# Two heads at a time in the row halves of the array, with fewer load slots

## The reference

```
layer 0: head size 32, scores = q k^T / sqrt(32) + causal mask - (pos_i - pos_j), gate silu(p) on the output
layer 1: head size 64, rotary q and k, four key/value heads shared by four query heads each
layer 3: head size 16, q and k from a low-rank projection
each:    o = softmax(scores) v, then the output projection
```

## Time and profile before

| | us |
|---|---|
| median of 3 runs | 4516.4 (4515.51 to 4525.6) |
| profiled execution | 4514.84 |
| its span | 4513.2 |
| PE busy, share of the span | 3375.2, 75% |
| DVE busy | 1985.5, 44% |
| ACT busy | 1256.6, 28% |
| mean granted TensorE clock | 0.866 |

### The profile page before, as it was taken

One profiled execution on the slowest core, in us unless ns is written; L12 is line 12 of the kernel. 1 busy time (PEld: TensorE's weight loads), 2 busy tenths in 40 slices (PEclk: granted clock), 3 DMA queues, 4 the chain that ended last, 5 costly groups with the idle time before them and its releaser, 6 DMA issues. The chain is left out here.

```text
span 4513.2 us, 51689 instructions
## 1 busy us (share of the span) xinstructions
PE 3375.2 (75%) x17778; PEld 1820.8 (40%) x17778; DVE 1985.5 (44%) x4344; ACT 1256.6 (28%) x1983; POOL 559.7 (12%) x610
## 2 busy tenths in 40 slices
PE   5799966777899567999974776855456887459676
PEld 2233333676555322333351454532332333222555
DVE  3466540432788654444413456223313774234212
ACT  3234421221354212333311300112112544224022
POOL 0101110000344231111100200001001001003100
PEclk9899988878899788999986978877687998679888
DMA  3302013112000232222222312223313111335243
GB/s 109 92 18 44 17 64 143 40 35 71 15 19 19 99 83 58 44 34 34 23 63 74 77 39 86 77 95 71 105 66 75 21 31 49 113 104 80 85 141 107
DMA packets 237902, 295.46 MB, mean 65 GB/s; under 512 B 69054, under 2 KB 182904, under 8 KB 235160
## 3 DMA queue, kind: packets, MB, share of 16 engines
q1 hardware_dynamic: 214360, 235.97, 18.1%
q0 software_dynamic: 23360, 57.11, 5.9%
HBM read 185.38 MB, written 104.73 MB: 64 GB/s over the span
## 5 line engine op out<-in xcount | busy, mean ns | idle before, releaser
L1007 DVE TENSOR_REDUCE l1a_nmax<-ps 128x1 f32<-128x512 f32 (+3 forms) x384 | 207.9, 556 | 219.6 <-PE ps L889 168.7
L2447 DVE SCALAR_TENSOR_TENSOR f_acc<-ps,f_gates,f_acc 128x256 f32<-128x256 f32 x672 | 278.0, 476 | 14.7 <-PE ps L2380 14.7
L991 ACT ACTIVATE l1a_probs<-ps 128x1024 f32<-128x1024 f32 x192 | 156.1, 813 | 379.8 <-PE ps L917 272.7
L2367 PE MATMUL ps<-f_x_parts,f_wf 128*128 128x512 f16 x1056 | 251.9, 382 | 7.5 <-DVE f_x_parts L2421 7.5
L1007 DVE TENSOR_REDUCE l0a_nmax<-ps 128x1 f32<-128x512 f32 (+3 forms) x384 | 200.9, 555 | 121.4 <-PE ps L889 92.5
L1007 DVE TENSOR_REDUCE l3a_nmax<-ps 128x1 f32<-128x512 f32 (+3 forms) x384 | 199.3, 553 | 80.7 <-PE ps L889 66.0
L991 ACT ACTIVATE l0a_probs<-ps 128x1024 f32<-128x1024 f32 (+1 forms) x192 | 145.5, 811 | 229.0 <-PE ps L917 181.4
L991 ACT ACTIVATE l3a_probs<-ps 128x1024 f32<-128x1024 f32 (+1 forms) x192 | 148.7, 809 | 184.1 <-PE ps L917 147.8
L2347 POOL TENSOR_TENSOR f_h_parts<-f_hid,f_h_parts 128x512 f16<-128x512 f32 x132 | 152.2, 1158 | 199.2 <-ACT f_h_parts L2400 199.2
L928 PE MATMUL ps<-l1a_probs,l_v_all 128*64 128x512 f32 (+3 forms) x768 | 166.7, 511 | 8.4 <-ACT l1a_sums L980 8.2
L889 PE MATMUL ps<-mask,ident_b 128*128 128x128 bf16 x768 | 169.5, 230 | 0.0
(11 more groups left out here) (696 smaller groups left out, 6457.9 us busy)
## 6 DMA issues: line engine op xcount, KB each, us to landing
f_w<-in_L_ffn_w_dram SPq DMA_DIRECT2D x16, 1024.0 KB, 7.2
x_qt<-x0p_st SPq DMA_DIRECT2D x16, 512.0 KB, 2.6
x0a_q<-x_qt SPq DMA_DIRECT2D x8, 1024.0 KB, 4.8
l1a_qs<-l_q_h SPq DMA_DIRECT2D x64, 128.0 KB
x3a_qs<-x_q_h SPq DMA_DIRECT2D x64, 128.0 KB
f_wf<-in_L_ffn_W_dram SPq DMA_DIRECT2D x99, 64.0 KB, 1.9
l0a_qs<-l_q_h SPq DMA_DIRECT2D x32, 128.0 KB
l0a_ks<-l_k_h SPq DMA_DIRECT2D x16, 256.0 KB
```

Of the source, the lines that this page charges most:

```text
L991: act.activation(probs[0:KR, n % SLOTS, 2 * pr:2 * pr + 2, 0:w], SB[x % 2][:, :, 0:w], ACT.Exp).then_inc(s_["exps"], 1)
L1007: dve.tensor_reduce(nmax[:, s % LEAD, f.chunk, f.p, f.tile:f.tile + f.n], src, AX.X, ALU.max, negate=True).then_inc(s_["maxed"], 1)
L2367: ins = pe.matmul(bank[i % 2], wf[:, s % 2, m, d * I:(d + 1) * I], x[:, d, g * GN:(g + 1) * GN], start=j == 0, stop=j == len(terms) - 1)
L2447: ins = dve.scalar_tensor_tensor(out=acc[:, t, :], in0=Y[i % 2][:, j, :], scalar=gates[:, t, ds(e + s, 1)], in1=acc[:, t, :], op0=ALU.mult ...
```

## The change

Three stacks are new, `TILED_32`, `TILED_64` and `TILED_16`, and the plans of the three attentions are paired. In the first pass heads are taken two at a time: the even head's q and k lie on partitions 0 to 63, the odd head's on 64 to 127, and each matmul uses its half of the rows. The two write to two banks; the mask matmuls of both follow, over the whole array. Only the high parts of q and k enter in layers 0 and 1 (38 and 64 rows). There the first pass has tiles of its own (`qa`, `ka`), loaded by 12 (layer 0) or 6 (layer 1) transfers ahead of the second-pass loads, with semaphores of their own (`a_ld`); `LOADS` becomes 2 there, and the two `SA` banks remain. In layer 3 the second pass is halved too: q and k have three parts per head on 48 rows plus the two rows of the maximum, both passes use the same tile, a load has 18 transfers and `maximum_rows` four; three `SA` banks, and one bank for the values instead of two; `LOADS` stays 3. `Plan.lay` hands out pairs instead of single maxima. SP's loop, quoted above, is unchanged.

```diff
+TILED_32 = Stack(32, STACK_32.q_parts, STACK_32.k_parts, [104], 38, 96, 102, 0, paired=True)
+TILED_16 = Stack(16, [(0, 0, "h"), (0, 16, "h"), (0, 32, "l")], [(0, 0, "h"), (0, 16, "l"), (0, 32, "h")], [64], 48, 32, 48, 0, q_fill=0.0, halved=True, paired=True)
+TILED_64 = Stack(64, STACK_64.q_parts, STACK_64.k_parts, [128, 128], 64, 64, 126, 1, q_fill=0.0, paired=True)
...
+            if self.paired:
+                n_max = len(todo) // 2 * 2
+                todo = [todo[i:i + 2] for i in range(0, n_max, 2)] + [[it] for it in todo[n_max:]]
+                cost = [0.3 + st.firsts[0].w / 450] * (n_max // 2) + [0.7] * (len(todo) - n_max // 2)
+            else:
+                todo = [[it] for it in todo]
...
-                beside[parts[-1][0]][parts[-1][1]].append(add(it))
+                    beside[n][k] += [add(it) for it in todo.pop(0)]
...
+                order = [(p + e, i) for p in range(0, G, 2) for i in range(gq) for e in range(2)] if paired else [(p, i) for p in range(G) for i in range(gq)]
...
-    LOADS = LEAD // 2 + 2
+    LOADS = 2 if stack.paired and not stack.halved else LEAD // 2 + 2
...
-    n_ld = len(stack.q_parts) * GB + len(stack.k_parts) + (GB + 1 if q_pos is not None else 0)
+    paired, halved = stack.paired, stack.halved
+    apart = paired and not halved
+    HB = 2 if halved else 1
+    n_ld = HB * (len(stack.q_parts) * GB + len(stack.k_parts)) + (GB + 1 if q_pos is not None else 0)
+    n_first = 2 * (GB + 1) * (2 if q_pos is not None else 1)
+    NSA = 3 if paired and own_sums else 2
...
-        qs = ph.sb("qs", [P, LOADS, C, GB, G, QC], F16)
-        ks = ph.sb("ks", [P, LOADS, KH, C, plan.n_keys], F16)
+        qs = ph.sb("qs", [P, LOADS, C, GB, G // HB, QC], F16)
+        ks = ph.sb("ks", [P, LOADS, KH // HB, C, plan.n_keys], F16)
+        KA = max(KH // 2, 1)
+        qa = ph.sb("qa", [P, LOADS, GB, G // 2, QC], F16) if apart else None
+        ka = ph.sb("ka", [P, LOADS, KA, plan.n_keys], F16) if apart else None
...
-        SA = [k.ps[:, i, :] for i in range(2)]
-        SB = [k.ps[0:KR, 2 + 2 * i:4 + 2 * i, :] for i in range(2)]
-        X = [k.ps[:, 6, :], k.ps[:, 7, :] if own_sums else k.ps[:, 6, :]]
+        SA = [k.ps[:, i, :] for i in range(NSA)]
+        SB = [k.ps[0:KR, NSA + 2 * i:NSA + 2 + 2 * i, :] for i in range(2)]
+        NX = 2 if own_sums and NSA == 2 else 1
+        X = [k.ps[:, 8 - NX if own_sums else 6, :], k.ps[:, 7, :] if own_sums else k.ps[:, 6, :]]
         Y = k.ps[:, 7, :]
-        NX = 2 if own_sums else 1
+        a_ld = [ph.sem(f"a_ld{i}") for i in range(LOADS)] if apart else ld
...
+                    if apart and tb >= LOADS:
+                        sp.wait_ge(s_["a_done"], turned_at[2 * (tb - LOADS) + 1])
+                    if q_pos is not None and tb < LOADS:
+                        sp.wait_ge(s_["k_filled"], slot + 1)
+                        sp.wait_ge(s_["q_filled"], slot + 1)
+                    for e in range(2 if apart else 0):
+                        rows = q["h"][h0 * dh:(h0 + G) * dh].rearrange("(h d) n -> d h n", d=dh)[:, e::2, :]
+                        k_rows = kk["h"][hk * dh:(hk + KH) * dh].rearrange("(h d) n -> d h n", d=dh)
+                        k_rows = k_rows[:, e::2, :] if KH > 1 else k_rows
+                        e0 = e * HALF
+                        for g in range(GB):
+                            sp.dma_start(qa[e0:e0 + dh, slot, g, :, :], rows[:, :, b * T + g * QC:b * T + (g + 1) * QC]).then_inc(a_ld[slot], 16)
+                        sp.dma_start(ka[e0:e0 + dh, slot, :, :], k_rows[:, :, b * plan.n_keys:(b + 1) * plan.n_keys]).then_inc(a_ld[slot], 16)
+                        if q_pos is not None:
+                            for g in range(GB):
+                                rows = q_pos[h0 + e:h0 + G:2, :, b * T + g * QC:b * T + (g + 1) * QC]
+                                sp.dma_start(qa[e0 + dh + 3:e0 + dh + 6, slot, g, :, :], rows.rearrange("h r n -> r h n")).then_inc(a_ld[slot], 16)
+                            sp.dma_start(ka[e0 + dh:e0 + dh + 3, slot, :, :], k_pos[h0 + e:h0 + G:2, :, b * T:(b + 1) * T].rearrange("h r n -> r h n")).then_inc(a_ld[slot], 16)
                     if tb >= LOADS:
                         sp.wait_ge(s_["b_done"], PR * plan.first_unit[2 * (tb - LOADS) + 2])
...
+                    for e in range(2 if halved else 0):
+                        e0 = e * HALF
+                        for c, r0, part in stack.q_parts:
+                            rows = q[part][h0 * dh:(h0 + G) * dh].rearrange("(h d) n -> d h n", d=dh)[:, e::2, :]
+                            for g in range(GB):
+                                sp.dma_start(qs[e0 + r0:e0 + r0 + dh, slot, c, g, :, :], rows[:, :, b * T + g * QC:b * T + (g + 1) * QC]).then_inc(ld[slot], 16)
+                        for c, r0, part in stack.k_parts:
+                            rows = kk[part][hk * dh:(hk + KH) * dh].rearrange("(h d) n -> d h n", d=dh)[:, e::2, :]
+                            sp.dma_start(ks[e0 + r0:e0 + r0 + dh, slot, :, c, :], rows[:, :, b * plan.n_keys:(b + 1) * plan.n_keys]).then_inc(ld[slot], 16)
+                    for c, r0, part in stack.q_parts if not halved else []:
...
+                        for e in range(2 if halved else 0):
+                            half = G * GQ // 2
+                            sp.dma_start(qs[e * HALF + R + i:e * HALF + R + i + 1, (s // 2) % LOADS, 0, st.q0 // QC, :, :],
+                                         m[e * half:(e + 1) * half, s % LEAD, :]).then_inc(m_ld[s % LEAD], 16)
+                        if halved:
+                            continue
...
+                    if halved:
+                        pool.memset(ks[stack.m0:HALF, i], 1.0)
+                    for e0 in (0, HALF) if q_pos is not None else ():
+                        pool.memset(ka[e0 + dh:e0 + dh + 6, i], 1.0)
+                    pool.memset(ks[P - HALF + stack.m0:P, i] if halved else ks[stack.m0:R + 2, i, :, stack.m_chunk, :], 1.0).then_inc(s_["k_filled"], 1)
...
-                            pe.wait_ge(s_["maxed"], a - 1)
+                            pe.wait_ge(a_ld[slot], 16 * (n_first if apart else n_ld) * (s // 2 // LOADS + 1))
+                        if a >= NSA:
+                            pe.wait_ge(s_["maxed"], a - NSA + 1)
                         f = st.firsts[i]
-                        for j in range(f.n):
+                        if paired:
+                            e0, g = (f.p % 2) * HALF, f.p // 2
+                            rows = slice(e0, e0 + stack.max_rows)
+                            left = qa[rows, slot, st.q0 // QC, g, f.tile * P:(f.tile + 1) * P] if apart else qs[rows, slot, 0, st.q0 // QC, g, f.tile * P:(f.tile + 1) * P]
+                            kg = g if KH > 1 else 0
+                            right = ka[rows, slot, kg, f.key:f.key + f.w] if apart else ks[rows, slot, kg, 0, f.key:f.key + f.w]
+                            ins = pe.matmul(sa[:, 0:f.w], left, right, start=True, stop=not f.masked)
+                            if f.masked and i % 2 == 0:
+                                return
+                            if f.masked:
+                                pe.matmul(SA[(a - 1) % NSA][:, f.w - P:f.w], k.ident_b[:], k.mask[:], start=False, stop=True).then_inc(s_["a_done"], 1)
+                        for j in range(0 if paired else f.n):
...
-                        pe.wait_ge(m_ld[s % LEAD], 32 * (s // LEAD + 1))
+                        pe.wait_ge(m_ld[s % LEAD], 32 * HB * (s // LEAD + 1))
+                        if apart and s % 2 == 0:
+                            pe.wait_ge(ld[slot], 16 * n_ld * (s // 2 // LOADS + 1))
...
+                        e0, g = place(p)
                         for d, r in enumerate(stack.rows):
-                            ins = pe.matmul(SB[x % 2][:, half, 0:w], ks[0:r, slot, p if KH > 1 else 0, d, u.key:u.key + KR],
-                                            qs[0:r, slot, d, st.q0 // QC, p, u.off:QC], start=d == 0, stop=d == C - 1 and not u.masked)
-                        if u.masked:
+                            ins = pe.matmul(SB[x % 2][:, half, 0:w], ks[e0:e0 + r, slot, g if KH > 1 else 0, d, u.key:u.key + KR],
+                                            qs[e0:e0 + r, slot, d, st.q0 // QC, g, u.off:QC], start=d == 0, stop=d == C - 1 and not u.masked)
+                        if u.masked and not halved:
                             ins = pe.matmul(SB[x % 2][:, half, 0:P], k.ident_b[:], k.mask_t[:], start=False, stop=True)
+                    for half in range(2 if u.masked and halved else 0):
+                        ins = pe.matmul(SB[x % 2][:, half, 0:P], k.ident_b[:], k.mask_t[:], start=False, stop=True)
...
+            packed_attention(k, "l0a", causal_plan(H, 4, True), 4, TILED_32, qt, kt, v_all, o_t, q_pos=q_pos, k_pos=k_pos, gate=gate)
+            packed_attention(k, "l1a", causal_plan(H, 2, True), 2, TILED_64, qt, kt, v_all, o_t, kv_of=H // KV)
```

(47 more changed lines are left out.)

18 lines of the change are left out of this document (5 added, 13 removed).

## The result

The median is 4749.1 us (4735.0 to 4765.4, four runs) against 4519.7: ratio 1.0508, 95% interval 1.0468 to 1.0548. The kernel is 5% slower.

The account below looks back on a forecast made before the run. PE was taken to bound layers 0 and 1, with some play in layer 3. Tiling -2, stalls +153 and slow clock +28 on 4514.8 gave 4694 us; range 4600 to 4785, the forecast's own 4630 to 4760.

Parts of the forecast that it names:

- The tiling by itself: All three attentions: saved stream against shape changes, bank waits and openings, without stalls or slow clock; sum -2 us.
- The stall: PE waits for late first-pass tiles in bodies: layer 1 14 x 6.9 us, layer 0 6 x 9.3; 153 together.
- The clock behind it: After each of 20 stalls in layers 0 and 1, PE runs at half clock, losing 1.4 us: 28 us.
- Changes of shape: More switches between row halves and full array in the three bodies, 0.094 us each: 74 us together.
- Saved stream: Two heads streaming at once save 0.16 us a pair: 27, 29 and 57 us in layers 0, 1 and 3.
- Waits for DVE: A pair takes both first-pass banks, so its second matmul waits for maxima: 18 us layer 0, 8 layer 1.
- the bank: Layer 3's third first-pass bank takes 10 us off its waits, between -25 and +15.
- the -18 of layer 3: Layer 3 gains 18 us: -57 stream, +41 shape changes, -10 third bank, +5 single values bank, +3 opening.
- Rival 1: Changes to row halves are free in all bodies, so 74 us are not paid: 4620 us; chance 0.12.
- rival 2: Row halves of a pair don't overlap, so the 113 us are not gained: 4807 us; chance 0.06.
- rival 3: First-pass loads in SP's queue arrive in time, no stalls or slow clock: 4485 us; chance 0.06.
- rival 4: Stalls in layers 0 and 1 occur but are cheap, 5 us each, clock untouched: 4613 us; chance 0.08.

Follow-up runs that it names:

- e1_early: The changed kernel with layers 0 and 1's first-pass tiles loaded one pair of steps earlier in SP's order: 4566.6 us.
- e6_paired_order: e3_bank with the changed kernel's order (heads alternating, maxima handed out two at a time), every matmul on the whole array: 4512.4 us.
- e3_bank: The kernel before, with only layer 3 given three first-pass banks and one values bank, no row halves: 4479.8 us.
- e2_only_l3: The changed kernel with layers 0 and 1 undone, so only layer 3 is changed: 4518.0 us.
- e4_early_reversed: e1_early with the widest tile of each head pair first, the 128-wide one last, in all three layers: 4525.6 us.
- e7_l3_first_only: The kernel before with row halves only in layer 3's first pass, on its own early-loaded tiles, second pass whole-array, three first-pass banks: 4520.7 us.
- e5_bank_reversed: e3_bank with each head's tiles widest first, 128 wide last, in all three layers, no row halves: 4463.1 us.

## Why the prediction was right, and where its sizes were off

The mechanism and the place of the loss were right: the late load and the slow clock behind it. The tiling by itself was put at -2 us and costs 46 to 49 (e1_early); that part of the sum was wrong, though small beside the rest. Profile against profile the loss is 220 us where 179 were forecast (layer 0 +84 for +83, layer 1 +143 for +114, layer 3 0 for -18).

- The stall: 6.9 us forecast for layer 1, 6.9 measured, 14 times; 96.4 us for 97. In layer 0 9.3 forecast, 7.3 measured, 43.8 us for 56: the landing was 1.7 us and not the 3.0 that I took from layer 1's opening, and the last issue came 4.5 us after the first and not 5.1. e1_early shows the cause.
- The clock behind it: 24.0 us in layer 1 and 14.8 in layer 0 for 20 and 8. After layer 0's stalls the slow stretch was 10.2 us, of which some 5 fell on working PE, not 2.8. Stalls and slow clock together are 179 us in the account for 181 forecast, and e1_early gives back 182; that this fits so well is partly luck, since the stalls were put 13 us too high and the clock 11 too low.
- Changes of shape: counted 183, 166 and 435 more, found 181, 164 and 416; 0.094 us each forecast, and the records show 0.105 out of a pair (0.318 us for 512 columns, 0.158 for 128) and 0.098 back. 83 us for 74. The drain that the Trainium skill names (TensorEngine Tiling (Array Packing), Tiling Modes) is there. Its doubling (the Trainium skill, same page, Theoretical Speedup) is also there for the pair by itself; a pair on a trip of its own from the full array must save 0.203 us, which takes 487 columns, and the mean here is 384.
- Saved stream: 86 us for 113. In layers 0 and 3 the second half of a pair often waits for a maximum, and its partner then streams alone: 15 and 44 for 27 and 57.
- Waits for DVE: +18 forecast in layer 0 and some 17 found. In layer 1, +8 forecast and some 25 found; this is a mis-sized term. I had counted only the next pair's second matmul and left out the turn. e6_paired_order shows that most of it is the order (19 us of stage), not the halves.
- Openings: +11, +2 and +3 us forecast for layers 0, 1 and 3; +9.0, -0.1 and -2.5 measured.
- Layer 3: the bank was put at 10 us, it is worth 37 (e3_bank), and the waits of pairs and the clock took it back. The slow clock there, 12 us, was not in the forecast at all. The forecast named a layer 3 slower than before as a sign of being wrong, and a body 20 us shorter as what would show it. The stage is 0.4 us shorter and its body 2 longer, and in e2_only_l3 the stage is 4.3 longer: the -18 of layer 3 is refuted.

Rival 1 falls by the 0.098 and 0.105 us, rival 2 by the 3 ns between the halves, rival 3 by the 20 waits, rival 4 by their length (6.5 to 7.3 us of idle PE) and by the clock at 0.50 behind them.

## What to carry to other kernels

When a slot is taken away, look at where the refill stands in its queue against the first instruction that needs it. A load issued after the last work of a step and wanted by the first of the next costs its issues and its landing each time (6.9 us in layer 1 here), although it moves fewer bytes. A pair of row halves among full-array matmuls gave back less than its stream: count the trips between shapes of the array, and take the pair only if it saves more stream than its trip costs. Parts of a change should be timed alone; here a spare bank worth 0.9% was hidden in a change that cost 5%, and with the widest tiles first, which is no part of the change, it is 1.1%.

## What the runs showed of the hardware that was not expected

In layer 3 TensorE's clock fell to the 1.2 GHz level with PE at work. The windows around one such stretch of the changed kernel, and every idle time of PE's matmuls up to it in its timeline:

```profile
3800.00:3807.70 7.70, 6.28 (x50) 2.45 (x50) 4.01 (x9) 1.79 (x4) 0.00 (x0) 1.00 0.24 64
3807.70:3814.50 6.80, 6.06 (x33) 1.25 (x32) 4.32 (x9) 4.56 (x5) 1.37 (x2) 0.50 0.23 51
3814.50:3822.00 7.50, 6.41 (x40) 1.44 (x36) 6.83 (x11) 3.99 (x4) 0.00 (x0) 1.00 0.00 0
```

```profile
3800.65 1.10 PE L974 MATMUL ps<-l3a_r_row,l3a_spread 128*128 128x512 f32 x2 [0.77 <-DMA l3a_r_row<-l3a_r_col]
3804.66 0.23 PE L954 MATMUL ps<-l3a_ks,l3a_qs 48*128 48x128 f16 x1 [0.57 <-DVE l3a_nmax L1088]
3807.34 0.33 PE L954 MATMUL ps<-l3a_ks,l3a_qs 48*128 48x384 f16 x1 [0.20 <-DVE l3a_nmax L1088]
```

No idle time there is longer than 0.77 us, and PE is 82% busy ahead of the fall. The changed kernel has five such stretches in that body (3.4 to 10.2 us, 31 in all), e1_early two, e2_only_l3 four, e4_early_reversed three, e7_l3_first_only two. The kernel before, e3_bank, e5_bank_reversed and e6_paired_order, with no row halves, have none that begins in that body, so neither the order of the tiles nor the bank brings them.

Nor do PE's waits by themselves, as a fall in e4_early_reversed and a stretch of the kernel before show (windows of both, in this order):

```profile
3573.80:3581.50 7.70, 7.01 (x62) 2.79 (x65) 4.73 (x12) 3.12 (x6) 0.00 (x0) 1.00 0.28 75
3581.50:3584.90 3.40, 3.40 (x22) 0.53 (x21) 2.00 (x5) 3.05 (x4) 1.38 (x2) 0.50 0.37 70
...
3696.30:3704.00 7.70, 5.88 (x51) 2.52 (x50) 5.75 (x14) 4.20 (x7) 0.83 (x2) 1.00 0.55 71
3704.00:3711.70 7.70, 7.01 (x35) 1.82 (x35) 6.52 (x11) 4.11 (x6) 0.54 (x1) 1.00 0.07 5
```

In e4_early_reversed PE is 91% busy ahead of the fall and never idle for over 0.39 us, and its other two falls look the same. The kernel before is 76% busy over as long a time and keeps the full clock. So the row halves are part of the cause. They are not all of it: layers 0 and 1 of e1_early have them in the first pass and show no fall in their bodies. What else layer 3 adds stays open.
